# Attention to output projection: heads 0 and 1 of the projection between the last products of attention

## The reference, cut to what matters

```
x = x + S4(attention(x))        # 32 query heads, 8 key heads, D = 128
x = x + ffn(cond(x))            # linear + LoRA, linear + 8 low-rank experts

attention: q, k, v = x @ Wq.T, x @ Wk.T, x @ Wv.T ; RMS norm, rotary positions
           keys and values of a cache (512 a sequence, by a block table) + 32 new ones
           o = softmax(q @ k.T * scale, masked) @ v
           return einsum('bse,de->bsd', o, Wo)      # the output projection, 4096 -> 512
S4:        K = kernel of 512 taps from Lambda, p, q, Vc, Ct, Bp, step   (no x in it)
           y = causal convolution of each row of 512 with K, + D * u
```

## Time and profile before

| | |
|---|---|
| median of 3 runs | 1321.12 us (1319.19 to 1321.59) |
| the profiled execution's own time | 1318.64 us |
| its span in the trace | 1316.9 us |
| TensorE busy | 1247.0 us (95%) |
| VectorE, ScalarE busy | 810.3 us each (62%) |
| GpSimd busy | 767.4 us (58%) |
| mean granted clock of TensorE | 0.982 |
| DMA | 214.84 MB, 162 GB/s over the span |
| chain that ended last, by engine | PE 81%, DVE 6%, issue 3%, DMA 3%, ACT 3% |

### The profile page before, as it was taken

How to read it: one execution, slowest core, us unless ns; L and a number is a source line. 1 busy time by engine, 2 the same in 40 slices (tenths; PEclk the granted TensorE clock), 3 DMA queues, 4 the chain that set the end, 5 groups by cost and what they waited for, 6 DMA issues and landing times.

```text
span 1316.9 us, 28777 instructions
## 1 busy us (share of the span) xinstructions
PE 1247.0 (95%) x7378; PEld 1040.4 (79%) x7378; DVE 810.3 (62%) x1724; ACT 810.3 (62%) x2256; POOL 767.4 (58%) x901
## 2 busy tenths in 40 slices
PE   6899969999999997998989999699999999999998
PEld 4678859998989985774757788599998989978856
DVE  5976647676776766772146866377676776755422
ACT  3676558788888873332135766478788888744330
POOL 3443448888888874543033434388888888854330
PEclk9999979999999998999989999899999999999999
DMA  7241388888888835305134321888888888333300
GB/s 244 88 137 64 111 233 229 233 239 240 233 234 234 235 78 179 134 0 190 35 110 133 113 96 64 247 227 228 238 243 241 234 236 231 112 107 134 96 33 33
DMA packets 148202, 214.84 MB, mean 163 GB/s; under 512 B 25940, under 2 KB 120470, under 8 KB 142102
## 3 DMA queue, kind: packets, MB, share of 16 engines
q1 hardware_dynamic: 128742, 202.75, 52.5%
q10 hardware_dynamic: 18576, 9.05, 2.5%
q0 software_dynamic: 800, 2.10, 0.5%
HBM read 203.33 MB, written 10.49 MB: 162 GB/s over the span
## 4 chain that ended last, share of the span: by engine, by line
PE 81%; DVE 6%; issue 3%; DMA 3%; ACT 3%; ACTq 2%; POOL 0%; SPq 0%; DVEq 0%; POOLq 0%
PE PS L1032 17%; PE PS L1000 9%; PE PS L931 4%; PE PS L927 4%; PE PS L923 4%; PE PS L1041 4%; PE PS L1092 3%; PE PS L1083 3%; PE PS L1089 3%; PE PS L967 2%; PE PS L1134 2%; PE PS L969 2%; PE PS L902 2%; PE PS L985 2%; PE PS L989 2%
## 5 line engine op out<-in xcount | busy, mean ns | idle before, releaser
L574 POOL TENSOR_TENSOR kv_parts<-kv,k_hi 128x544 fp32r<-128x544 f32 x192 | 258.7, 1348 | 41.6 <-ACT k_hi L765 40.0
L1032 PE MATMUL PS<-probT,kv 128*128 128x128 f32 x2048 | 270.4, 275 | 0.0
L527 POOL TENSOR_TENSOR ring_parts<-ring,kv_parts 128x512 fp32r<-128x512 f32 x96 | 128.0, 1341 | 227.4 <-ACT kv_parts L641 227.4
L1032 PEld LDWEIGHTS PS<-probT,kv 128*128 128x128 f32 x2048 | 248.8, 192 | 0.1
L1492 DVE COPY probT<-PS 128x512 f32<-128x512 f32 x256 | 175.5, 686 | 3.1 <-PE PS L1000 3.1
L804 ACT ACTIVATE ring<-ring,smin 128x544 f32<-128x544 f32 x192 | 143.8, 749 | 38.3 <-DVE smin L1486 37.2
L1486 DVE CUSTOM_DVE_ANT_0 ring<-PS,mask,rq 128x544 f32<-128x544 f32 x192 | 150.0, 781 | 21.9 <-PE PS L990 13.8
L765 ACT ACTIVATE k_hi<-kv 128x544 fp32r<-128x544 f32 x192 | 125.9, 657 | 52.4 <-PE PS L990 48.8
L605 POOL TENSOR_TENSOR ring_parts<-ring,kv_parts 128x512 fp32r<-128x512 f32 x64 | 89.1, 1397 | 105.8 <-ACT kv_parts L844 105.8
L562 POOL TENSOR_SCALAR ring<-ring,rinv 128x512 f32<-128x512 f32 x192 | 133.6, 696 | 0.0
L923 PE MATMUL PS<-kv_parts 128*128 128x512 f32 x384 | 115.0, 419 | 16.8 <-ACT kv_parts L641 14.2
(11 more groups left out here) (214 smaller groups left out, 2738.9 us busy)
## 6 DMA issues: line engine op xcount, KB each, us to landing
kv<-in_kpages SPq DMA_DIRECT2D x512, 128.0 KB, 2.3
kv<-in_vpages SPq DMA_DIRECT2D x496, 128.0 KB, 3.3
ring<-in_w SPq DMA_DIRECT2D x46, 1024.0 KB, 4.9
kv<-in_xT SPq DMA_DIRECT2D x4, 1024.0 KB, 8.8
v_new<-kv ACTq DMA_DIRECT2D x64, 64.0 KB, 2.5
k_new<-kv ACTq DMA_DIRECT2D x16, 256.0 KB, 2.3
kv<-k_new SPq DMA_DIRECT2D x32, 128.0 KB, 2.7
kv<-v_new SPq DMA_DIRECT2D x32, 128.0 KB, 2.4
```

The costliest lines, as they stand in the source:

```text
L574: nc.gpsimd.tensor_tensor(kbuf_lo(par)[:, :, g, :], kbuf(par)[:, :, g, :], k_hi[:, e % 2, :].rearrange("p (j t) -> p j t", t=PSIZE), ALU.s ...
L1032: mm = nc.tensor.matmul(PS[:, at:at + D], vbuf(bpar)[:, c, gg * D:(gg + 1) * D], probT[:, g % 2, c * P:(c + 1) * P], start=(c == 0 and a = ...
```

## The change

On TensorE the projection of a head becomes a function, `project_part(head)`, with unchanged instructions. Heads 0 and 1 are called earlier: head 0 between `values(HB - 1, 1, HK - 2)` and `values(HB - 1, 1, HK - 1)`, head 1 between that and the last `values_new`. Head 0 first waits until VectorE has read the last scores from banks 0 to 3 (`masked`) and until all but the last `keep_o` are done. Heads 2 and 3 follow the last `values_new`; head 4 waits for the last `keep_o`.

On ScalarE the high parts of one head become `upper_part(head)`. The order at the end of attention was: `spread_new`, `keep_o` of the first group, `keep_o` of the second group, high parts of heads 0, 1, 2 and so on. It becomes: `keep_o` of the first group, high parts of head 0, `spread_new`, high parts of head 1, `keep_o` of the second group, high parts of heads 2, 3 and so on. GpSimd, VectorE and SyncE keep their programs.

```diff
-                spread_new(HB - 1, 1)
-                keep_o(HB - 1, 0)
-                keep_o(HB - 1, 1)
-
-
-                act.wait_ge(ot_read, QUADS * (h + 1))
-                for head in range(HQ):
+                def upper_part(head):
+
                     n, a = head // 4, head % 4
...
+                keep_o(HB - 1, 0)
+                act.wait_ge(ot_read, QUADS * (h + 1) - 1)
+                upper_part(0)
+                spread_new(HB - 1, 1)
+                upper_part(1)
+                keep_o(HB - 1, 1)
+                act.wait_ge(ot_read, QUADS * (h + 1))
+                for head in range(2, HQ):
+                    upper_part(head)
...
-                values(HB - 1, 1, HK - 2, False)
-                values(HB - 1, 1, HK - 1, False)
-                values_new(HB - 1, 1, 1, False)
-
-
-                pe.wait_ge(ot_read, QUADS * (h + 1))
-                for head in range(HQ):
+                def project_part(head):
+
                     n, a = head // 4, head % 4
...
+                values(HB - 1, 1, HK - 2, False)
+                pe.wait_ge(masked, STEPS * (h + 1))
+                pe.wait_ge(ot_read, QUADS * (h + 1) - 1)
+                project_part(0)
+                values(HB - 1, 1, HK - 1, False)
+                project_part(1)
+                values_new(HB - 1, 1, 1, False)
+                for head in range(2, 4):
+                    project_part(head)
+                pe.wait_ge(ot_read, QUADS * (h + 1))
+                for head in range(4, HQ):
+                    project_part(head)
```

More of the change, by code:

```diff
@@ L1106, in _ @@
                             transform()
+                turn_probs(HB - 1, HK - 2, False)
+                values(HB - 1, 1, HK - 3, False)
+                turn_probs(HB - 1, HK - 1, False)
+                turn_new(HB - 1, 1, False)
+                values(HB - 1, 1, HK - 2, False)
[10 more added lines that the diff above has]
+                    project_part(head)
                 pe.wait_ge(u_ready, 4 * h + 4)
```

## The result

The changed kernel takes 1325.32 us, the median of 20 runs (1322.17 to 1328.49), against 1321.46 us (1317.88 to 1323.85) of 20 runs of the kernel before beside it: 3.9 us slower, ratio 1.003 with a 95% interval of 1.0021 to 1.0038. The direction and the path were as forecast; the size was not, since 5.6 us were forecast.

The account below looks back on a forecast made before the run. TensorE was busy 95% of the span, but the first half was taken as bound by attention's last product through dft's landing to VectorE. First half 5.6 plus second half 0, on 1321.12, gave 1326.7 us, range 1323.8 to 1330.4.

Parts of the forecast that it names:

- No hole to fill, and 5.6 us later: TensorE at attention's end: two heads of 2.79 us fill only a 0.14 us hole, so the last product ends 5.6 us later.
- ScalarE's first part costs nothing: ScalarE ahead of spread_new: first group's keep_o and two high parts, 1.85 us, fit into 2.55 us of idle time; 0 us.
- The idle time is moved, not filled: TensorE behind the last product: the 2.1 us wait for ScalarE comes again, now before head 2; 0 us.
- The low clock behind it: Behind the seam's idle time in both halves: the fall to 0.50, costing 1.5 us, comes again; 0 us, bounds 1.5 either way.
- The landing sets the first half: SyncE issues dft after the last product, so it lands 5.6 us later, at 514.2, and VectorE starts steps then.
- Its price, 5.6 us: First half: everything behind the landing keeps its distance to the last product, so the half is 5.6 us longer.
- That term: Clock behind head 6, first half: less idle time may prevent its fall, up to 1.4 us gained; taken as nothing.
- the low bound: Smallest loss of the likeliest case: 5.6 less 1.5 for no clock fall and 1.4 at head 6, 2.7 us.
- The second half, 0 us: Second half: two heads done earlier, seam starts 5.6 us later, two heads fewer follow, later DMAs hidden; 0 us.
- The hidden landing: Rival, first half: dft's landing doesn't bind, both seams come out at zero, 1321.1 us; chance 0.10.
- The closed seam: Rival: head 2's high parts are ready when values_new ends, saving 4.7 us a seam; 1311.7 us if both gain, chance 0.04.
- Two stalls more: Rival: lower(0) slowed beside GpSimd and spread_new 1.85 us late, in both halves; 1332 us, chance 0.06.

Follow-up runs that it names:

- e3: Changed kernel with both values and values_new ahead of heads 0 and 1, last eviction awaited only before head 2: 5.9 us faster than before by medians, ratio 0.9962.
- e8: Changed kernel with head 1 moved behind values_new, only head 0 between the values: 2.1 us faster than before, ratio 0.9985.
- e9: Kernel before with VectorE's computation of the S4 kernel left out, same DMAs issued: ratio 0.9942 to before.
- e10: Changed kernel with VectorE's computation of the S4 kernel left out: ratio 0.9948 to before.
- e7: Kernel before with the dft DMA issued later, behind the LoRA matrices of two sequences: 4.5 us slower by medians, 4.0 by the ratio.
- e5: Changed kernel with dft issued early, 18.1 us ahead of the end of the last product: 1324.56 us, median 3.1 us above before.
- e6: e3 with dft issued early: 6.6 us faster than before, ratio 0.995.
- e11: e3 with dft early and the five small tensors issued ahead of weight block 15: 7.3 us below before in medians, ratio 0.9944.
- e1: The changed kernel run again without edit, for a second profile: 4.1 us slower than the kernel before.
- e4: Kernel before with dft issued early, 12.3 us ahead of the end of the last product: 1319.80 us, median 1.7 us faster than before.
- e2: ScalarE's new order alone, TensorE in its old order and awaiting the last eviction before head 0: 6.2 us faster by medians, ratio 0.9955.

## Why the prediction was right, and where its size was off

**No hole to fill, and 5.6 us later.** Right. The last product is 5.7 us later in the first half and 5.9 in the second. `lower(0)` took 0.71 us in the first half (alone, as taken), and the stall behind it was 0.2 us.

**ScalarE's first part costs nothing.** Right: `keep_o` of the first group started 0.39 us into the idle time, and `spread_new` started 0.25 us later than before, which is the shift of the whole trace.

**The idle time is moved, not filled.** Right in both halves, 2.04 us for 2.13, by the three instructions named. The low clock behind it did not come in both, as was taken: in the first half of the first profile it stayed away, and in the second half it lasted twice as long. e3 and e8 show what its removal is worth, and e9 and e10 that the move itself is worth nothing.

**The landing sets the first half.** Right in its mechanism: 12.9 us from the last product to the landing, e7 makes the same loss without moving a matmul, and without VectorE's work the loss is gone (e9, e10). Too narrow in its cause: e5 shows that the small tensors, issued behind the same wait, bind as soon as `dft` doesn't.

**Its price, 5.6 us, was mis-sized: 2.7 and 3.0 us.** The prediction's own sign of being wrong, a first half that isn't 5 to 6 us longer, came true. I had written that everything behind the landing keeps its distance. Head 3 did (5.6 us later), head 6 came 3.9 us later, the convolution 2.7. Two terms give back. The clock stayed up behind head 6, where TensorE waited 0.74 us and not 4.05: 7 slow matmuls fewer, 1.3 us (3.9 less 2.7). That term stood in the prediction as a bound and was valued at nothing. The other, 1.6 us between head 3 and head 6, was not in it. That the total stayed in the range in spite of it is in part luck: the low bound had 1.5 us in it for a seam without a fall of the clock, which is not what made the difference. From head 3 to head 6 it took 12.70 us before (510.66 to 523.36), on VectorE's path, and takes 11.07. Line L1522 of before and L1535 of after, in the stretch behind `steps`:

```profile
L1522 DVE TENSOR_TENSOR qo_parts<-qo,kv_parts x3: 678/693/1780, 509.9 to 512.2; 128x512 fp32r<-128x512 f32 x3
```

```profile
L1535 DVE TENSOR_TENSOR qo_parts<-qo,kv_parts x3: 684/685/693, 515.7 to 516.9; 128x512 fp32r<-128x512 f32 x3
```

One of three `lower` took 1.78 us beside GpSimd, now none does: 1.1 us. In `denominators` two instructions took 1.40 instead of 0.42 us before (L1283 and L1287); now one does, and another takes 0.86: 0.5 us. One of these rows of before, with GpSimd's beside it, then in the trace of after ScalarE's next high part behind the stall and GpSimd's next row:

```profile
514.66 1.40 DVE L1283 TENSOR_TENSOR kv<-kv,consts 128x256 f32<-128x256 f32 x1
...
514.35 1.43 POOL L605 TENSOR_TENSOR ring_parts<-ring,kv_parts 128x512 fp32r<-128x512 f32 x1 [2.60 <-ACT kv_parts L844]
```

```profile
521.05 0.63 ACT L839 ACTIVATE kv_parts<-ring 128x512 fp32r<-128x512 f32 x1 [11.98 <-PE PS L1079]
...
521.86 1.40 POOL L605 TENSOR_TENSOR ring_parts<-ring,kv_parts 128x512 fp32r<-128x512 f32 x1 [11.87 <-ACT kv_parts L839]
```

TensorE's longer stall at head 3 had stopped GpSimd, whose next L605 came only at 521.86, so VectorE ran alone until then. By these rows GpSimd waits for ScalarE there, and ScalarE for a matmul of TensorE. The rule that the prediction weighed for `lower(0)` (the Trainium skill, SBUF — State Buffer, section "Who interferes with whom": a VectorE instruction with two SBUF inputs and a GpSimd instruction that reads SBUF exclude each other) applied elsewhere, and with the other sign. These rows agree with it: 0.42 and 0.69 us alone, 1.40 and 1.78 beside L605.

Both terms stand in every trace that has VectorE as releaser at both heads. A short stall at head 3 leaves GpSimd running and gives nothing back; a long one gives back both:

```
            idle at    from head 3   idle at    clock behind
            head 3 us  to head 6 us  head 6 us  head 6
before      1.33       12.70         4.05       0.50
e5          1.12       12.68         4.06       0.50
e6          0.91       12.68         4.06       falls to 0.50
e11         0.90       12.68         4.04       falls to 0.50
the change  8.37       11.07         0.74       1.00
e1          7.67       11.23         0.69       1.00
e3          6.04       10.75         0.74       1.00
e7          6.73       10.98         0.74       1.00
```

This is also why e5 loses 4.5 us against e4 in the profiles and the change only 2.7 against before. In e4 and e5 alike GpSimd runs beside `denominators`, with two instructions at 1.40 us. Head 6 comes 3.4 us later in e5, and behind it the clock falls in e5 (4.06 us idle) and not in e4 (2.69 us idle).

**The second half, 0 us.** 1.7 in one profile, 0.1 in the other; the bound of 1.5 us for a longer low clock was about right. 2.7 to 3.0 and 0.1 to 1.7 make 3.1 to 4.4 us, and the medians say 3.9 and 4.1. As said above, the stages are differences to one trace of before.

**The rivals.** The hidden landing is refuted by e7 and by e9 with e10. The closed seam did not happen in the change, but its price was right: 4.5 us in the second half of e3 against 4.7 worked out. Two stalls more did not come: `lower(0)` ran alone, and `spread_new` was not late.

## What to carry to other kernels

When work is moved ahead of the last producer of a stage, look at everything that waits for this producer, DMAs of other engines included: the move delays it by its whole length. How much of the delay is paid depends on what the engines do meanwhile: here a longer stall of TensorE let VectorE run undisturbed and kept the clock up later, and gave half of it back. A wait on an engine's order is not filled by running the other engine's work earlier; it goes when work whose operands are finished is kept back for it. Here the same two heads, with their operands made early but run behind the last product, turned 3.9 us lost into 6 us gained.

## What the runs showed of the hardware that I had not expected

The granted clock answers to the same idle time differently from one execution to the next. Idle times of 2.04 and 0.4 us behind the last product were followed by none (after, first half), 6 (e1, second half), and 14 slow matmuls (after, second half). Over all 13 traces 2.04 or 2.13 us of idle time stand at 16 seams. Behind 14 of them the clock fell, behind 2 it did not (after, first half, and e7, second half). At the 10 seams with 0.77 us or none (e2, e3, e6, e8, e11) it never fell. The second halves that the change's code gives lie between 97.65 and 99.26 us, and those of before's code between 96.43 and 97.98. So a single profile of such a seam is uncertain by some 1.6 us.
